# Delta rule in four quadrants of TensorE: products of two neighbouring tiles interleaved, odd tiles' products crossed to the other half of the partitions

## The reference, cut to what matters

```python
S = S * exp(g_t)
delta = (v_t - k_t @ S) * b_t
S = S + outer(k_t, delta)
o_t = q_t @ S
```

## Time and profile before

| | us |
|---|---|
| median of 3 runs | 553.33 (552.94 to 554.77) |
| the profiled execution's own time | 552.51 |
| its span | 550.7 |
| TensorE (PE) busy | 472.1, 86% |
| TensorE weight loads (PEld) busy | 342.5, 62% |
| VectorE (DVE) busy | 371.9, 68% |
| ScalarE (ACT) busy | 259.6, 47% |
| GpSimd (POOL) busy | 255.1, 46% |

### The profile page before, as it was taken

One profiled execution on the slowest core, in us unless ns is written; L12 is line 12 of the kernel. 1 busy time (PEld: TensorE's weight loads), 2 busy tenths in 40 slices (PEclk: granted clock), 3 DMA queues, 4 the chain that ended last, 5 costly groups with the idle time before them and its releaser, 6 DMA issues.

```text
span 550.7 us, 15538 instructions
## 1 busy us (share of the span) xinstructions
PE 472.1 (86%) x5648; PEld 342.5 (62%) x5648; DVE 371.9 (68%) x896; ACT 259.6 (47%) x659; POOL 255.1 (46%) x338
## 2 busy tenths in 40 slices
PE   4969898758688999999868999986999699999665
PEld 2434343324377989999746767764456488888554
DVE  0658495659958656666756889996484177777536
ACT  1448574635582444444537676672211044444316
POOL 0227230425502866663555555455788035656600
PEclk9979999959988999999979999999799899999969
DMA  8991000004855480100375000001148625553284
GB/s 283 277 296 5 0 0 0 2 0 149 278 157 110 106 226 22 60 4 4 79 288 236 2 3 2 3 33 52 71 159 297 190 74 164 165 177 120 88 311 156
DMA packets 62451, 64.00 MB, mean 116 GB/s; under 512 B 31460, under 2 KB 52012, under 8 KB 62124
## 3 DMA queue, kind: packets, MB, share of 16 engines
q1 hardware_dynamic: 57964, 50.19, 29.6%
q0 software_dynamic: 3840, 10.75, 5.3%
q10 hardware_dynamic: 576, 2.10, 1.3%
HBM read 37.01 MB, written 28.25 MB: 119 GB/s over the span
## 4 chain that ended last, share of the span: by engine, by line
PE 49%; DVE 26%; POOL 6%; issue 6%; ACT 5%; DMA 5%; SPq 2%; POOLq 0%; ACTq 0%; DVEq 0%
PE ps L1174 7%; DVE work L1617 6%; PE ps L731 5%; PE ps L953 4%; POOL slots_dr L2249 4%; PE ps L1191 4%; PE ps L721 4%; DVE work L1796 4%; DVE arena L1800 3%; PE ps L934 2%; PE ps L896 2%; PE ps L885 2%; PE ps L907 2%; PE ps L919 2%; ACT arena L1453 2%
## 5 line engine op out<-in xcount | busy, mean ns | idle before, releaser
L1617 DVE SCALAR_TENSOR_TENSOR work<-ps,colp,work 96x504 f32<-96x504 f32 (+5 forms) x84 | 59.5, 729 | 22.3 <-ACT work L1248 20.3
L2283 POOL DMA_INDIRECT rows_dr<-work,dest_i x48 | 46.0, 959 | 50.1 <-DVE work L2049 30.3
L731 PE MATMUL ps<-xT,front 128*96 128x512 f32 (+3 forms) x112 | 50.7, 597 | 0.0
L1174 PE MATMUL ps<-vsg,work 128*128 x192 | 50.5, 386 | 0.0
L721 PE MATMUL ps<-front,work 128*128 128x396 f32 x64 | 28.5, 601 | 14.8 <-ACT ab L1241 7.8
L2191 POOL TENSOR_TENSOR arena<-front,consts 128x384 f32<-128x384 f32 x32 | 26.6, 835 | 30.0 <-DMA front<-inverse_dr 24.6
L2034 DVE TENSOR_TENSOR work<-ps,xT 128x256 f32<-128x256 f32 x48 | 20.4, 424 | 23.2 <-PE ps L1174 23.2
L1554 ACT ACTIVATE work<-work 128x128 f32<-128x128 f32 x48 | 14.8, 309 | 43.8 <-DVE work L2034 43.8
L731 PEld LDWEIGHTS ps<-xT,front 128*96 128x96 f32 (+1 forms) x112 | 19.1, 177 | 26.3 <-issue 25.9
L2249 POOL DMA_INDIRECT slots_dr<-xn,slots_i x32 | 31.3, 977 | 8.8 <-issue 5.0
L2117 POOL TENSOR_TENSOR work<-arena 96x512 f32<-96x512 f32 (+1 forms) x16 | 16.5, 1040 | 40.2 <-ACT arena L1259 40.2
(11 more groups left out here) (248 smaller groups left out, 1262.1 us busy)
## 6 DMA issues: line engine op xcount, KB each, us to landing
work<-slots_dr SPq DMA_DIRECT2D x48, 136.0 KB, 2.2
vsg<-wexp_dram SPq DMA_DIRECT2D x4, 1536.0 KB, 12.5
vsg<-rows_dr SPq DMA_DIRECT2D x8, 512.0 KB, 7.6
blocks_dr<-work SPq DMA_DIRECT2D x16, 192.0 KB, 2.7
mats_dr<-work SPq DMA_DIRECT2D x8, 384.0 KB, 3.2
work<-mats_dr SPq DMA_DIRECT2D x3, 768.0 KB, 5.6
slots_dr<-zero SPq DMA_DIRECT2D x8, 272.0 KB
pads_dr<-zero SPq DMA_DIRECT2D x8, 272.0 KB
```

The source lines that it names most:

```text
L731: mm = pe.matmul(ps[0:ROWS[j], BANK[j], :], wc3[:, k, CH0[j]:CH0[j] + ROWS[j]], xT3[:, k, bass.ds(g * GT, GT)], start=(k == 0), stop=(k == ...
L1174: mm = pe.matmul(ps[:, 2 + j % 2, 0:2 * F], xgT[:, j % 2, k, :], wres[:, bass.ds(e + k * 2 * F, 2 * F)], start=(k == 0), stop=(k == KD - 1))
L1617: dve.scalar_tensor_tensor(y[:, :, d:T], z[:, :, 0:T - d], taps[0:r, j, KSZ - 1 - d:KSZ - d], y[:, :, d:T], ALU.mult, ALU.add).then_inc(s_ ...
L2283: pool.indirect_dma_start(out=rows_dr, out_offset=bass.IndirectOffsetOnAxis(ap=dest_i[:, j:j + 1], axis=0), in_=yob[:, j % YO, :], in_offs ...
```

## The change

Odd tiles write some products to the other half of the partitions, and a later product writes back. `couple_first` of an odd tile crosses, so `u1` has its sequences swapped; `couple_second` crosses back, with a copy of `mt` whose halves are swapped (two DMAs per odd tile from SBUF to SBUF, `cross_couplings`, in SyncE's list). `solve` of an odd tile from tile 5 on crosses, so `vt` is swapped, and `attend` crosses back, with attention matrices that `load_attention` already loads swapped for odd tiles (three DMAs in place of one). `couple_inverses` and `couple_third` never cross. On TensorE the groups of a step are taken in twos (`attend` with `solve`, `couple_third` with `couple_second`, `couple_first` with `couple_inverses`), head by head, with the waits of both ahead of the first product. Their operands, banks and semaphores are otherwise as before.

```diff
+        mt_crossed = [front[:, F_WG + 384 * u:F_WG + 384 * (u + 1)].rearrange(by_head, h=H) for u in range(2)]
+        def chain_crosses(n):
+            return n % 2 == 1
+        def solution_crosses(n):
+            return n % 2 == 1 and n >= GP
+        halves_of = [slice(T * z, T * z + T) for z in range(2)]
+        s_mc_in = s_out
...
                 if g >= 2:
                     sp.wait_ge(s_o, at(GP * (g - 1)))
-                sp.dma_start(att[g % 2].rearrange("p m h t -> p m (h t)"),
-                             mats_dr[GP * g:GP * (g + 1), :, 0:H * T].rearrange("n p c -> p n c")).then_inc(s_att_in[g % 2], 16)
+                here, there = att[g % 2].rearrange("p m h t -> p m (h t)"), mats_dr[GP * g:GP * (g + 1), :, 0:H * T]
+                sp.dma_start(here[:, 0::2], there[0::2].rearrange("n p c -> p n c")).then_inc(s_att_in[g % 2], 16)
+                for z in range(2):
+                    sp.dma_start(here[halves_of[z], 1::2],
+                                 there[1::2, halves_of[1 - z]].rearrange("n p c -> p n c")).then_inc(s_att_in[g % 2], 16)
+            def cross_couplings(n):
+                u = n // 2 % 2
+                sp.wait_ge(s_mk, at(n + 1))
+                if n >= 4:
+                    sp.wait_ge(s_a2, at(n - 3))
+                for z in range(2):
+                    sp.dma_start(mt_crossed[u][halves_of[z]], mt[n % 4][halves_of[1 - z]]).then_inc(s_mc_in[u], 16)
...
             load_inverses(0, 1)
+            cross_couplings(1)
+            load_couplings(2)
+            cross_couplings(3)
             sp.wait_ge(s_ka, at(TURNED[1]))
             store_inverses(1, 1, nt_flat)
             store_inverses(0, 1, nb_flat)
-            load_couplings(2)
             sp.wait_ge(s_inv_out[1][1], 32)
             load_inverses(1, 2)
+            cross_couplings(5)
             load_attention(1)
             sp.wait_ge(s_inv_out[1][0], 32)
             load_inverses(0, 2)
             load_inverses(1, 3)
+            cross_couplings(7)
             load_couplings(3)
             load_attention(2)
+            cross_couplings(9)
             load_inverses(0, 3)
+            cross_couplings(11)
             load_attention(3)
+            cross_couplings(13)
+            cross_couplings(15)
+            sp.wait_ge(s_a2, at(NT))
             sp.wait_ge(s_np[0], at(NT))
...
+            def couple_first(n, h):
+                for z, r in enumerate(halves_of):
+                    mm = pe.matmul(ps[out_of(z, chain_crosses(n)), 5, h * DV:(h + 1) * DV], mt[n % 4][r, h, :],
+                                   vt[r, n * HV + h * DV:n * HV + (h + 1) * DV], start=True, stop=True)
...
+            def before_second(n):
                 pe.wait_ge(s_u1, at(n + 1))
+                if chain_crosses(n):
+                    pe.wait_ge(s_mc_in[n // 2 % 2], 32 * (n // 4 + 1))
...
             for i in range(-5, NT + 2):
                 if 0 <= i < NT:
-                    attend(i)
+                    before_attend(i)
                 if 0 <= i + 1 < NT:
-                    solve(i + 1)
+                    before_solve(i + 1)
+                for h in range(H):
+                    if 0 <= i < NT:
+                        attend(i, h)
+                    if 0 <= i + 1 < NT:
+                        solve(i + 1, h)
...
```

More of the change, by code:

```diff
@@ L859, in _, with out_of, before_inverses @@
             keep_clock(3, 32)
-            sequences = [slice(T * s, T * s + T) for s in range(2)]
-            def couple_inverses(n):
-                g, m = divmod(n, GP)
+            def out_of(z, crosses):
+                return halves_of[1 - z] if crosses else halves_of[z]
+            def before_inverses(n):
+                g = n // GP
                 if g >= 2:
@@ L870, in couple_inverses, with before_first @@
                     pe.wait_ge(s_mk, at(n))
-                for h in range(H):
-                    for r in sequences:
-                        mm = pe.matmul(ps[r, 4, h * T:(h + 1) * T], nx[r, 1, n % 2, h, :], cpl[g % 2][r, m, h, :],
-                                       start=True, stop=True)
-                mm.then_inc(s_mt, 1)
-            def couple_first(n):
+            def couple_inverses(n, h):
+                g, m = divmod(n, GP)
+                for r in halves_of:
+                    mm = pe.matmul(ps[r, 4, h * T:(h + 1) * T], nx[r, 1, n % 2, h, :], cpl[g % 2][r, m, h, :],
+                                   start=True, stop=True)
+                if h == H - 1:
+                    mm.then_inc(s_mt, 1)
+            def before_first(n):
                 pe.wait_ge(s_mk, at(n + 1))
@@ L904, in couple_third, with before_solve @@
                     pe.wait_ge(s_v2, at(n))
-                for h in range(H):
-                    for r in sequences:
-                        mm = pe.matmul(ps[r, 7, h * DV:(h + 1) * DV], mt[n % 4][r, h, :],
-                                       vt[r, n * HV + h * DV:n * HV + (h + 1) * DV], start=True, stop=True)
-                mm.then_inc(s_a3, 1)
-            def solve(n):
+            def couple_third(n, h):
+                for r in halves_of:
+                    mm = pe.matmul(ps[r, 7, h * DV:(h + 1) * DV], mt[n % 4][r, h, :],
+                                   vt[r, n * HV + h * DV:n * HV + (h + 1) * DV], start=True, stop=True)
+                if h == H - 1:
+                    mm.then_inc(s_a3, 1)
+            def before_solve(n):
                 pe.wait_ge(s_v2, at(n + 1))
@@ L916, in solve, with before_attend @@
                     pe.wait_ge(s_w, at(n))
-                for h in range(H):
-                    for r in sequences:
-                        mm = pe.matmul(ps[r, 0, h * DV:(h + 1) * DV], nx[r, 0, n % 2, h, :],
-                                       vt[r, n * HV + h * DV:n * HV + (h + 1) * DV], start=True, stop=True)
-                mm.then_inc(s_w0, 1)
-            def attend(n):
+            def solve(n, h):
+                for z, r in enumerate(halves_of):
+                    mm = pe.matmul(ps[out_of(z, solution_crosses(n)), 0, h * DV:(h + 1) * DV], nx[r, 0, n % 2, h, :],
+                                   vt[r, n * HV + h * DV:n * HV + (h + 1) * DV], start=True, stop=True)
+                if h == H - 1:
+                    mm.then_inc(s_w0, 1)
+            def before_attend(n):
                 g = n // GP
                 if g >= 1:
-                    pe.wait_ge(s_att_in[g % 2], 16 * ((g + 1) // 2))
+                    pe.wait_ge(s_att_in[g % 2], 48 * ((g + 1) // 2))
                 pe.wait_ge(s_w, at(n + 1))
@@ L930, in attend @@
                     pe.wait_ge(s_og, at(n))
-                for h in range(H):
-                    for s in range(2):
-                        r = slice(64 * s, 64 * s + 64)
-                        mm = pe.matmul(ps[r, 1, h * DV:(h + 1) * DV], att[g % 2][r, n % GP, h, :],
-                                       vt[r, n * HV + h * DV:n * HV + (h + 1) * DV], start=True, stop=True)
-                mm.then_inc(s_o, 1)
+            def attend(n, h):
+                for z, r in enumerate(halves_of):
+                    mm = pe.matmul(ps[out_of(z, solution_crosses(n)), 1, h * DV:(h + 1) * DV], att[n // GP % 2][r, n % GP, h, :],
+                                   vt[r, n * HV + h * DV:n * HV + (h + 1) * DV], start=True, stop=True)
+                if h == H - 1:
+                    mm.then_inc(s_o, 1)
             def turn_heads(n):
```

45 lines of the change are left out of this document (27 added, 18 removed).

## The result

| | median, us | runs | range |
|---|---|---|---|
| before | 555.38 | 20 | 552.94 to 560.28 |
| after | 549.53 | 20 | 546.27 to 552.61 |

The ratio is 0.990, 95% interval 0.987 to 0.992: 5.6 us faster where 15.3 were forecast, and outside the range of 535 to 546. Run once more on the chip of the last experiments the changed kernel gave 0.987 (0.984 to 0.991). The profiled execution took 546.58 us (span 544.5).

A forecast was written before the change was run, and what follows sets the result against it. TensorE was taken to bound the delta rule's middle steps. 16.1 us from crossed pairs, less 0.4 for late inverses and 0.4 for the tail, gave 15.3 off 552.5: 537.2, median 538.0 us; range 535 to 546.

The forecast's parts named there:

- Crossed pair 0.70: Delta rule on TensorE: a crossed pair of groups costs 0.70 us instead of 1.40, a middle step 4.76 instead of 6.16.
- A: Rival for crossed pairs: no overlap on shared rows, pairs stay at 1.40 us, kernel 553.5 us; chance 0.07.
- B: Rival for crossed pairs: half the overlap, a pair costs 1.05 us, kernel 545.6 us; chance 0.07.
- The pair there is crossed, 0.70 instead of 1.56, so it ends when it did: Fill, couple_third(0)'s pair: tile 1's copy lands about 179.2 against a start at 178.30, and the shorter pair makes that up.
- Tile 3's copy: Fill: copy queued behind the couplings lands about 186.9, wanted at 186.7; taken as 0, with 1 us lateness in the range.
- Instruction supply: TensorE's instruction packets: one stop of 1.29 us kept as before, so 0, with −1.3 and +2.6 us for the range.
- Rival C: TensorE starved of instructions, a stop with every packet from step 3 on: 22 us lost, kernel 560 us; chance 0.06.
- Rival D: Crossed copies late at every odd tile, needing to land 9.6 us after the mask to eat the gain; chance under 0.02.
- SyncE's list: Reordered and added DMAs and waits on SyncE's queue: neutral or better, taken at nothing, hidden behind TensorE's steps.
- Order within pairs: Both groups' waits ahead of the first product: bites in step 2, solve(3) awaiting GpSimd's inverses, 0.4 us off the gain.
- Tail: Before the last projections: TensorE's waits for ScalarE's copies grow by 0.4 us, between 0 and 1.4.
- 16.1 us of TensorE time: Largest term, delta rule: 23 crossed pairs that count, each 0.70 us shorter, give 16.1 us.

The follow-up runs named there:

- e2: Changed kernel with nothing crossed and no crossed copies, SyncE's list and attention load as before; only the interleaving left: 557.08 us, ratio 1.006.
- e4: Changed kernel with only solve and attend of odd tiles crossed, coupling chain uncrossed, no crossed copies: 548.87 us, ratio 0.992.
- e7: Changed kernel with 48 idle matmuls ahead of TensorE's wait for tile 1's crossed copy: 544.37 us, ratio 0.984.
- e8: Changed kernel with tile 3's crossed copy ahead of the load of couplings(2) on SyncE's list: 545.20 us, ratio 0.985.
- e1: Changed kernel with couplings crossed only from tile 5 on and couplings(2) loaded behind the inverses' stores again: 544.71 us, ratio 0.983.
- e5: e1 with the load of couplings(2) put back ahead of the stores of the inverses: 543.71 us, ratio 0.983.
- e3: Kernel before plus idle TensorE instructions, which were not in the program that ran, so before's code again: 552.66 us, one run.
- e6: e5 with the projection's three wide matmuls spread, one behind each pair of groups in a step: 546.05 us, ratio 0.986.

## Why the prediction was wrong

**Crossed pair 0.70: right.** A crossed pair takes 0.68 to 0.71 us off a step, and e2 and e4 show that crossing is the whole of it: no crossed pair 6.16 us, one 5.48, two 4.78. Rivals A and B are out. With A falls the rule of the Trainium skill ("TensorE: Matmul & The Clock Gate", Part 3, What overlaps and what doesn't) for this case: crossed quadrants share both row groups, and PEld is busy 4.45 of 4.89 us under them.

**"The pair there is crossed, 0.70 instead of 1.56, so it ends when it did": wrong, 2.6 us.** Two errors in one sentence. The copy landed 4.2 us after its issue and not 3 after the mask, which cost 1.0 us. And I priced idle time as idle time alone: the clock that fell behind it cost 1.6 more (e7).

**Tile 3's copy, "I take 0 for it and put 1 us of lateness into the range": 0.9 us.** As its high end had it, and for the reason given, the couplings ahead on the queue (e8).

**Instruction supply: the step that failed most, 4.2 us.** I had the stop's cause, and then averaged the consumption over a step, "the new middle step in about 3.8", and set no time for a fetch beside it. Instructions do not come averaged, and neither do fetches. The three blocks of steps 4 to 6 that ran dry were gone in 4.24, 2.77 and 3.74 us, where the next one took 5.0, 3.6 and 4.5 to come: 0.8 us of stop each. In the fill there are no projections to thin the stream out, and the loads slow the fetch: 0.62, 0.95 and 1.72 us. I kept one stop; there are six, 5.7 us against 1.5. Rival C named the mechanism with a wrong frequency: it decides from 0.9 us a packet at every packet, and it came at six packets of sixteen with 0.95 on average. Rival D didn't come: from tile 5 on TensorE waits for no copy. (Its 9.6 us are worked out from no row.)

**SyncE's list "neutral or better": right, and for a reason I didn't see.** The couplings ahead of the stores save 2.2 us at the stop of 3198 and lose 0.6 at the next (e1 against e5).

**Order within pairs, 0.4: not where I had put it.** The late inverses don't show as a wait; step 2 began at 195.5 and not 192.8, for the stops ahead. What the order cost was in the fill, 0.9 us (e2 against e3), and before's own half clock there made up for it.

**Tail, 0.4: right.** TensorE waits for ScalarE's copies at four projections and not two, and the steps 13 and 14 last 0.2 us each more than their pairs give, though the waits' sum is 1.7 us against 1.6 in the earlier trace rows.

The sum: 2.6 + 0.9 + 4.2 = 7.7 of the 8.0 us missing in the stage. Behind attend(0) the steps took 1.1 us more than their pairs and stops give, among them 4.78 to 4.97 in place of 4.76 and the tail, where I had set 0.8 aside; that is the rest. The sign, the overlap of crossed pairs and the largest term were right; nearly half of the 16.1 us of TensorE time that the crossing freed went into waits, 3.5 us around the crossed copies and 4.2 into stops for instructions.

## What to carry to other kernels

When an engine is made to work off its instructions faster, look at the densest stretch of 256, not at the mean: 96 small matmul and weight load records in 0.70 us leave a block in 2.5 to 2.8 us, and where TensorE stopped the next one came 3.6 us after entry with quiet DMA queues and 4.4 to 5.0 with loads in flight. Not every such block stops, for a packet can begin early. Wide instructions thin the stream, but don't scatter them for that: here the switches cost 6.5 us to save 2.4 of stops; rather keep large loads out of the dense stretches. And idle time of TensorE can cost twice, once as a wait and once through the clock behind it: 1.6 us behind the wait of 3.3 for tile 1's copy, 1.3 and about 1.5 behind the stops of 2.8 and 2.9 us in e8 and e1, and nothing behind e4's of 2.6. So where a transfer is late in a pipeline's fill, begin such a scheme a tile or two later, where the copies have cover.

## What was unexpected

- A stop for instructions stays at its count of records when work is added ahead (57 of 57). What makes the fetch of a block begin stays open: in after's last steps one packet began 0.4 us before the block ahead of it was entered, others 0.6 to 1.6 us behind it.
- That loads delay the fetch is shown by moving one (2.87 to 0.68 us at the same count, in one profile each; 2.64 to 2.91 in the three kernels that have it behind the stores and cross or interleave, 0.38 to 0.96 in the ones that have it ahead), how they do isn't. The Trainium skill ("DMA: Bandwidth & Descriptors", Queues, rings and completion order) has a DMA engine serve its queues in turn, a packet at a time; no run here shows that for q8.
- One excursion from 64×64 to full-width matmuls and back costs 0.35 us on TensorE (e6).
- Twice 96 KB from SBUF to SBUF landed 4.2 us after the first issue for tile 1, where a single one has a median of 2.8 over all sixteen; a 192 KB store takes 2.1.
